# A ternary feed-forward layer: its second product from three bf16 parts of the squared activations instead of one f32 matmul

## What is computed

```python
def _ternary_weight(w, group_size):
    wb = w.astype(jnp.bfloat16)
    wg = wb.reshape(-1, group_size)
    scale = jnp.clip(jnp.mean(jnp.abs(wg), axis=-1, keepdims=True), 1e-08, None)
    q = jnp.clip(jnp.round(wg / scale), -1.0, 1.0)
    qs = (q * scale).reshape(w.shape).astype(w.dtype)
    return w + jax.lax.stop_gradient(qs - w)
...
w1 = _ternary_weight(W_fc, GROUP)             # 1024 x 256
h = jnp.einsum('bsd,hd->bsh', x, w1)
h = jnp.square(jax.nn.relu(h))                # 2048 x 1024
hn = _rms_norm(h)
w2 = _ternary_weight(W_proj, GROUP)           # 256 x 1024
return jnp.einsum('bsh,dh->bsd', hn, w2)
```

## Time and profile before

| | us |
|---|---|
| median of 3 runs (1603.28 to 1605.0) | 1603.55 |
| the profiled execution, device time | 1604.46 |
| its span from the first to the last instruction | 1602.7 |
| first `up` of the ternary layer / last `down` ends | 927.5 / 1050.3 |
| busy in the span: PE / DVE / ACT / POOL | 1513.1 / 1035.5 / 780.7 / 358.5 |

### The profile page before, as it was taken

The page is one execution under the profiler, slowest core; times in us unless marked ns, Lnnn a source line. Parts: engine busy times, 40 slices in busy tenths (PEclk is TensorE's granted clock), DMA queues, the critical chain, the costliest instruction groups (busy, mean ns, idle before and its releaser), DMA issues.

```text
span 1602.7 us, 35635 instructions
## 1 busy us (share of the span) xinstructions
PE 1513.1 (94%) x14908; PEld 943.9 (59%) x14908; DVE 1035.5 (65%) x1872; ACT 780.7 (49%) x1797; POOL 358.5 (22%) x403
## 2 busy tenths in 40 slices
PE   7999788999989999899999989999999999999998
PEld 4667454444444443445656557777777777764556
DVE  3678777788888883623436965367787878842223
ACT  2431446667767776341111153376767767732110
POOL 2322000000100003200000044335545555630000
PEclk9999889999999999999999999999999999999999
DMA  6000231000000003010000040000000020000000
GB/s 193 2 2 8 79 83 20 12 13 10 13 4 13 3 13 115 8 54 3 16 0 0 1 132 1 7 1 8 1 8 1 2 90 1 2 0 1 14 13 27
DMA packets 31823, 39.05 MB, mean 24 GB/s; under 512 B 7531, under 2 KB 26607, under 8 KB 31151
## 3 DMA queue, kind: packets, MB, share of 16 engines
q1 hardware_dynamic: 31662, 36.77, 7.9%
HBM read 23.79 MB, written 2.10 MB: 16 GB/s over the span
## 4 chain that ended last, share of the span: by engine, by line
PE 76%; DVE 11%; issue 4%; DMA 3%; ACT 3%; POOL 1%; SPq 1%; POOLq 0%; DVEq 0%; ACTq 0%
PE PS L1493 7%; PE PS L1499 7%; PE PS L1522 7%; PE PS L2742 6%; PE PS L1263 6%; PE PS L1218 6%; PE PS L1249 5%; DVE arena L1402 4%; PE PS L2249 4%; PE PS L2729 3%; PE PS L2707 3%; DMA arena<-arena 3%; PE PS L341 2%; PE PS L2572 2%; PE PS L2219 2%
## 5 line engine op out<-in xcount | busy, mean ns | idle before, releaser
L1332 ACT ACTIVATE arena<-PS 128x512 f32<-128x512 f32 (+3 forms) x640 | 313.9, 534 | 135.9 <-PE PS L1249 57.6
L1402 DVE TENSOR_REDUCE arena<-PS 128x1 f32<-128x1024 f32 (+7 forms) x320 | 326.6, 1059 | 58.1 <-PE PS L1221 41.2
L1249 PE MATMUL PS<-arena 99*32 99x512 bf16 (+3 forms) x2560 | 212.3, 352 | 1.5 <-ACT arena L1332 1.0
L1218 PE MATMUL PS<-arena 96*32 96x512 bf16 (+3 forms) x2560 | 185.2, 358 | 25.4 <-DVE arena L1402 24.4
L1263 PE MATMUL PS<-arena 128*32 128x512 f32 (+3 forms) x1280 | 150.1, 542 | 2.4 <-ACT arena L1338 1.7
L192 POOL TENSOR_TENSOR rstd<-ve,mhalf 128x4 f32<-128x4 f32 x31 | 31.7, 1023 | 498.5 <-DVE ve L220 498.4
L1218 PEld LDWEIGHTS PS<-arena 96*32 96x32 bf16 x2560 | 63.7, 98 | 103.5 <-DVE arena L1402 53.3
L2893 ACT ACTIVATE arena<-arena 128x128 f32<-128x128 f32 x256 | 122.7, 484 | 0.0
L1493 PE MATMUL PS<-XT,arena 128*128 128x512 f32 x256 | 120.4, 592 | 0.9 <-DVE arena L1730 0.9
L2742 PE MATMUL PS<-arena 128*128 128x256 f32 x512 | 121.0, 379 | 0.2
L1499 PE MATMUL PS<-XT,arena 128*128 128x512 f32 x256 | 120.3, 592 | 0.0
(11 more groups left out here) (250 smaller groups left out, 2692.7 us busy)
## 6 DMA issues: line engine op xcount, KB each, us to landing
arena<-arena SPq DMA_DIRECT2D x79, 128.0 KB, 2.4
XT<-in_L_attn_xT SPq DMA_DIRECT2D x4, 512.0 KB, 7.8
X<-in_L_attn_x SPq DMA_DIRECT2D x4, 512.0 KB, 9.5
arena<-in_L_attn_out_w SPq DMA_DIRECT2D x1, 2048.0 KB, 8.3
out<-X SPq DMA_DIRECT2D x3, 512.0 KB, 3.0
arena<-in_dmask SPq DMA_DIRECT2D x1, 1024.0 KB, 5.8
arena<-in_L_ffn_W_up SPq DMA_DIRECT2D x1, 1024.0 KB, 5.0
arena<-in_L_ffn_W_gate SPq DMA_DIRECT2D x1, 1024.0 KB, 7.5
```

The source lines that it names most:

```text
L1218: last = pe.matmul(flat[p, o:o + w], q[:, p], a.KS[0:SROWS, CH * kc:CH * kc + w], start=True, stop=kc < c)
L1249: last = pe.matmul(PS[p, b, lo:CH], keys[:, p], a.QS[0:rows, G1 * g + r, CH * c + lo:CH * (c + 1)], start=True, stop=j < TPC * c)
L1332: act.activation(a.PB[:, n % 3, r, lo:CH], PS[:, 4 + x % 3, lo:CH], ACT.Exp, scale=D0 ** -0.5).then_inc(a.e2, 1)
L1402: dve.tensor_reduce(dst, src, AX.X, ALU.max, negate=True).then_inc(a.m1, 1)
```

## The change

1. `a.down` is bf16: q * scale * sign, without the two f32 steps (subtract w, add w) that followed for the second weight matrix.
2. The f32 h of a tile is kept in 3 tile buffers instead of two whole chunks, and is split into three bf16 parts, whose sum is h: ACT makes the high part as the square of r (`l2f_high`), DVE the residual h - high (`l2f_residual`), POOL the middle part by a cast of the residual (`l2f_middle`), DVE the low part, residual - middle (`l2f_low`).
3. down is 3 bf16 matmuls in place of each f32 one. It waits for `low_s` (by halves) instead of h.
4. h(n) on DVE also waits for the square and the residual of tile n - 3; relu(n) also for the high part of tile n - 2. The DVE order is h(n), residual(n - 1), low(n - 2); the ACT order relu(n), high(n), square(n - 1); the POOL order middle(n - 1), add(n).
5. The gated layers (fourth and eighth) share one set of semaphores, with an offset `a.n0` in the counts.

```diff
@@ l2f_alloc
-    a.h = v(10 * n, [P, 2, HT, CH])
+    a.parts = [[v(at, [P, HT, CH], BF16) for at in slot] for slot in ((9216, 18944, 20992), (24640, 26688, 14400))]
+    a.h = v(12288, [P, 3, CH])
+    a.res = v(23040, [P, 2, CH])
-    a.down = a.q[:, 1, :].rearrange("p (t e) -> p t e", t=HT)
+    a.downb = v(6720, [P, n], BF16)
+    a.down = a.downb.rearrange("p (t e) -> p t e", t=HT)
@@ ternary_dve
-    elif step == 2:
+    else:
         dve.wait_ge(a.wb_s, 4 * m + 2 + half + 1)
-        last = dve.tensor_tensor(sign if m == 0 else q, q, sign, ALU.mult)
-    elif step == 3:
-        last = dve.tensor_tensor(q, q, w, ALU.subtract)
-    else:
-        last = dve.tensor_tensor(q, q, w, ALU.add)
+        last = dve.tensor_tensor(sign if m == 0 else a.downb[:, cols], q, sign, ALU.mult)
@@ l2f_relu
     if n >= 2:
         act.wait_ge(a.h_s, n - 1)
+        act.wait_ge(a.high_s, n - 1)
@@ new, and l2f_hidden
+def l2f_high(k, act, n):
+    act.wait_ge(a.r_s, n + 1)
+    if c >= 2 and it == 0:
+        act.wait_ge(k.f_ready, NC * 5 + c - 1)
+    act.activation(a.parts[c % 2][0][:, it, :], a.r[:, n % 2, :], ACT.Square).then_inc(a.high_s, 1)
+def l2f_residual(k, dve, n):
+    dve.wait_ge(a.high_s, n + 1)
+    dve.wait_ge(a.h_s, n + 1)
+    if n >= 2:
+        dve.wait_ge(a.low_s, n - 1)
+    dve.tensor_tensor(a.res[:, n % 2, :], a.h[:, n % 3, :], a.parts[c % 2][0][:, it, :], ALU.subtract).then_inc(a.res_s, 1)
+def l2f_middle(k, pool, n):
+    pool.wait_ge(a.res_s, n + 1)
+    pool.tensor_copy(a.parts[c % 2][1][:, it, :], a.res[:, n % 2, :]).then_inc(a.mid_s, 1)
+def l2f_low(k, dve, n):
+    dve.wait_ge(a.mid_s, n + 1)
+    dve.tensor_tensor(a.parts[c % 2][2][:, it, :], a.res[:, n % 2, :], a.parts[c % 2][1][:, it, :], ALU.subtract)\
+       .then_inc(a.low_s, 1)
 def l2f_hidden(k, dve, n):
     dve.wait_ge(a.r_s, n + 1)
-    if c >= 2 and it == 0:
-        dve.wait_ge(k.f_ready, NC * 5 + c - 1)
-        dve.wait_ge(a.sq_s, HT * (c - 1))
+    if n >= 3:
+        dve.wait_ge(a.sq_s, n - 2)
+        dve.wait_ge(a.res_s, n - 2)
@@ l2f_pe
     def down(c, j, half):
+        if j == 0:
+            pe.wait_ge(a.low_s, HT * c + HT // 2 * (half + 1))
         for it in range(HT // 2 * half, HT // 2 * (half + 1)):
-            last = pe.matmul(f_tile(k, j), a.h[:, c % 2, it, P * j:P * (j + 1)], a.down[:, it, :],
+            for part in range(3):
+                last = pe.matmul(f_tile(k, j), a.parts[c % 2][part][:, it, P * j:P * (j + 1)], a.down[:, it, :],
@@ l2f_act, before the loop over chunks
+    l2f_high(k, act, 0)
+    l2f_high(k, act, 1)
@@ l2f_pool, squares(c)
         for it in range(1, HT):
+            l2f_middle(k, pool, HT * c + it - 1)
             pool.wait_ge(a.sq_s, HT * c + it + 1)
@@ l2f_dve, hidden(c)
             if n >= 3:
                 l2f_hidden(k, dve, n)
+            if n >= 1:
+                l2f_residual(k, dve, n - 1)
+            if n >= 2:
+                l2f_low(k, dve, n - 2)
+            if n == HT * NC - 1:
+                l2f_residual(k, dve, n)
+                l2f_low(k, dve, n - 1)
+                l2f_low(k, dve, n)
@@ l3_front_act
-    act.wait_ge(k.l2f.h_s, HT * NC)
+    act.wait_ge(k.l2f.low_s, HT * NC)
```

More of the change, by code:

```diff
@@ L1471, in l1_dve, with glu_alloc @@
     dve.wait_ge(k.xn_done, 3 * NC)
-def glu_alloc(k, a, name, o):
+def glu_alloc(k, a, layer, o):
     a.h = k.view(o, [P, 2, HT, CH])
@@ L1480, in glu_alloc @@
     s = k.sem
-    a.g_mm, a.u_mm = s(name + "_gate_projected"), s(name + "_up_projected")
-    a.sil_s, a.h_s = s(name + "_silu"), s(name + "_hidden")
+    a.n0 = HT * NC * layer
+    a.g_mm, a.u_mm = s("gate_projected"), s("up_projected")
+    a.sil_s, a.h_s = s("gate_silu"), s("gated_hidden")
 def glu_up(k, pe, a, s, c, it):
     PS = k.PS
-    n = HT * c + it
+    n = a.n0 + HT * c + it
     if it == 0:
@@ L1516, in glu_pe @@
         else:
[L1517 removed]
+            pe.wait_ge(a.h_s, a.n0 + HT * NC)
         pe.wait_ge(k.r_done, NC * s + c)
@@ L1636, in l1f_alloc @@
     a.down = v(18944, [P, HT, E])
-    glu_alloc(k, a, "l1f", 21000)
+    glu_alloc(k, a, 0, 21000)
     a.ld = k.sem("l1f_ld")
@@ L2061, in l2f_alloc @@
     n = KT * HID
-    a.q = v(2 * n, [P, 2, n])
+    a.q = v(2 * n, [P, n])
     a.w = v(4 * n, [P, 2, n])
@@ L2094 @@
                (1, 0): (1, 0, 0), (1, 1): (1, 0, 1), (1, 6): (1, 1, 0), (1, 7): (1, 1, 1), (2, 0): (1, 2, 0), (2, 1): (1, 2, 1)}
-TERNARY_DVE = [(0, step, half) for step in range(3) for half in range(2)] + [(1, step, half) for step in range(5) for half in range(2)]
+TERNARY_DVE = [(0, step, half) for step in range(3) for half in range(2)] + [(1, step, half) for step in range(3) for half in range(2)]
 def ternary_sp(k, sp, I):
@@ L2228, in l2f_relu @@
         act.wait_ge(a.h_s, n - 1)
+        act.wait_ge(a.high_s, n - 1)
     act.activation(a.r[:, n % 2, :], k.PS[:, n % 2, :], ACT.Relu).then_inc(a.r_s, 1)
+def l2f_high(k, act, n):
+    a = k.l2f
+    c, it = n // HT, n % HT
+    act.wait_ge(a.r_s, n + 1)
[3 more added lines that the diff above has]
+def l2f_residual(k, dve, n):
+    a = k.l2f
+    c, it = n // HT, n % HT
+    dve.wait_ge(a.high_s, n + 1)
[4 more added lines that the diff above has]
+def l2f_middle(k, pool, n):
+    a = k.l2f
+    c, it = n // HT, n % HT
+    pool.wait_ge(a.res_s, n + 1)
+    if c >= 2 and it == 0:
+        pool.wait_ge(k.f_ready, NC * 5 + c - 1)
+    pool.tensor_copy(a.parts[c % 2][1][:, it, :], a.res[:, n % 2, :]).then_inc(a.mid_s, 1)
+def l2f_low(k, dve, n):
+    a = k.l2f
+    c, it = n // HT, n % HT
+    dve.wait_ge(a.mid_s, n + 1)
+    dve.tensor_tensor(a.parts[c % 2][2][:, it, :], a.res[:, n % 2, :], a.parts[c % 2][1][:, it, :], ALU.subtract)\
+       .then_inc(a.low_s, 1)
 def l2f_hidden(k, dve, n):
     a = k.l2f
-    c, it = n // HT, n % HT
     dve.wait_ge(a.r_s, n + 1)
-    if c >= 2 and it == 0:
-        dve.wait_ge(k.f_ready, NC * 5 + c - 1)
-        dve.wait_ge(a.sq_s, HT * (c - 1))
+    if n >= 3:
+        dve.wait_ge(a.sq_s, n - 2)
+        dve.wait_ge(a.res_s, n - 2)
     r = a.r[:, n % 2, :]
-    dve.tensor_tensor(a.h[:, c % 2, it, :], r, r, ALU.mult).then_inc(a.h_s, 1)
+    dve.tensor_tensor(a.h[:, n % 3, :], r, r, ALU.mult).then_inc(a.h_s, 1)
 def l2f_pe(k, pe):
@@ L2247, in down @@
     def down(c, j, half):
+        if j == 0:
+            pe.wait_ge(a.low_s, HT * c + HT // 2 * (half + 1))
         for it in range(HT // 2 * half, HT // 2 * (half + 1)):
-            last = pe.matmul(f_tile(k, j), a.h[:, c % 2, it, P * j:P * (j + 1)], a.down[:, it, :],
-                             start=it == 0, stop=it == HT - 1)
+            for part in range(3):
+                last = pe.matmul(f_tile(k, j), a.parts[c % 2][part][:, it, P * j:P * (j + 1)], a.down[:, it, :],
+                                 start=(it, part) == (0, 0), stop=(it, part) == (HT - 1, 2))
         if (j, half) == (TPC - 1, 1):
@@ L2300, in square @@
             dst = a.sq[:, it % 2, :]
-        act.activation(dst, a.h[:, c % 2, it, :], ACT.Square).then_inc(a.sq_s, 1)
+        act.activation(dst, a.h[:, n % 3, :], ACT.Square).then_inc(a.sq_s, 1)
+    l2f_high(k, act, 0)
+    l2f_high(k, act, 1)
     for c in range(NC):
@@ L2307, in l2f_act @@
                 l2f_relu(k, act, n)
+                l2f_high(k, act, n)
             if it >= 1:
@@ L2327, in squares @@
         acc = a.acc[:, c % 2, :]
+        if c >= 1:
+            l2f_middle(k, pool, HT * c - 1)
         for it in range(1, HT):
+            l2f_middle(k, pool, HT * c + it - 1)
             pool.wait_ge(a.sq_s, HT * c + it + 1)
@@ L2344, in l2f_pool @@
             squares(c + 1)
+            if c + 1 == NC - 1:
+                l2f_middle(k, pool, HT * NC - 1)
         else:
```

13 lines of the change are left out of this document (7 added, 6 removed).

## The result

The median went from 1603.41 us to 1637.32 us (four runs, 1636.89 to 1638.03), a ratio of 1.021 (95% interval 1.0192 to 1.0228): 33.9 us slower, where 1634.0 with a range of 1614 to 1656 was forecast. The profiled execution has a span of 1635.1 us, 32.4 more than before.

A forecast was written before the change was run, and what follows sets the result against it. DVE and POOL, taking turns at a shared SBUF resource, were to bound the ternary layer instead of PE: +32 for the later last down, -4 saved there, +2 for clock, 1604.5 + 30 less 0.9 = 1634 us, range 1614 to 1656.

The forecast's parts named there:

- PE's part: Ternary layer's down: 128 f32 matmuls of 432 ns become 384 bf16 ones of 107 ns, saving 14.2 us of PE.
- the weight loads: Rival in down: weight loads pace the bf16 matmuls at 205 ns, giving 1658 us; chance 0.04.
- the rival in which PE stays the bound: DVE and POOL run side by side in the ternary layer, so all 14.2 us are saved: 1589 us; chance 0.09.
- The step that decides: Ternary layer: DVE and POOL exclude each other, so a tile holds their shared resource 3.32 us against PE's 2.58.
- The second rival: POOL's cast doesn't take turns with DVE: 2.85 us a tile, 15.0 us less, 1619 us; chance 0.09.
- The sum: Held times from the third tile to low(31) total 113.9 us; last down begins at 1056.2 instead of 1024.22, +32.0.
- DVE's list is unbroken from the third tile on: DVE starts the third tile's product about 938.7, is free at 940.5, then works without a break to low(31).
- The named new waits of h(n) and relu(n): Ternary layer: these added waits are on things a full tile old, so they were given no cost.
- The last chunk: After the last down begins, faster matmuls save 4 us and the lowered clock after PE's gap costs 2.
- the third rival: PE falls to 1.2 GHz, +36 us for three chunks, 1670; chance 0.12 beyond 1655; sign: layer clock below 0.9.
- The tail doesn't wait for down: In each chunk down is done 16.3 us after its second half starts, within the 19.9 us DVE has left.
- Where the cover went: Forecast cover: PE's chunk needs 22.3 us, DVE with POOL 25.5 plus a 6.25 tail, so PE's saving counts only last.

The follow-up runs named there:

- the filler kernel: Changed kernel plus throwaway PE matmuls, 16 before the low-part wait in chunks 0 to 2 and 30 before the last down: 1633.53 us beside 1602.79, ratio 1.0189.

## Why the prediction was right

**PE's part** held: twelve bf16 matmuls take 1.31 us (109 ns each; 107 was taken), and the weight loads set no pace. The removal of the splitting gave 1591, near the 1589 of the rival in which PE stays the bound.

**The step that decides** held: DVE's two-input products and POOL's reading operations take turns, a tile at 3.29 us (3.32), the cast among them. The cast's turn, 0.47 in the sum, measured as 0.41 when it was taken away and 0.42 when it was doubled. The second rival (a free cast, 1619) falls by both runs and by the steady rows, where h takes 1.09 us beside a cast.

**The sum** was 2.5 us short at the last down: 1058.7, not 1056.2. low(31) ended at 1057.0, not 1054.4. Some 0.5 of it was there before the splitting began: the first h starts at 931.96, where it was 931.45, and so the third at 939.2, not 938.7. The step that failed is "DVE's list is unbroken from the third tile on". DVE waited 8.6 us for relu, and only the first 2.4 were in the sum; 6.2 came later. The prediction checked down(c) against DVE's tail alone. But on PE the `up` of the next tiles stands behind the down that waits for the low part, so when that down starts late and at half clock, relu is late and DVE runs out of work (2.08 us at 1005.83). The named new waits of h(n) and relu(n) aren't what held: those relus waited for PE's `up`.

Of these 6.2 us and the 0.5, some 4 were made good. A tile 0.03 us shorter than forecast explains 0.9. The rest can be read from the rows after such a wait, POOL first:

```profile
1007.06 1.80 POOL L2378 TENSOR_TENSOR arena<-arena 128x512 f32<-128x512 f32 x1 [2.84 <-ACT arena L2341]
```
```profile
1008.43 0.97 DVE L2278 TENSOR_TENSOR arena<-arena 128x512 f32<-128x512 f32 x1 [0.71 <-ACT arena L2232]
```

The addition ran mostly while DVE waited, and held h up for 0.29 us only, not for the 1.14 of the sum. Three additions (972.99, 1007.06, 1038.33) did so, and two casts (1003.21, 1035.02) ran wholly in such waits: by the held times of the sum that is 3 x 0.85 + 2 x 0.47 = 3.5 us, an estimate. How much of the 6.2 us is the clock, no run tells; the filler kernel, which gives 0.6 us back at that point, kept the clock up in one of three chunks.

The step from the profile to the median added to the miss: 0.9 was taken off for it, while the profiled execution of the changed kernel lay 0.4 below its median (1636.89 and 1637.32). Both are within what executions differ by.

**The last chunk** made good 2.1 us; -4 + 2 = -2 was forecast. The 2 us for the clock are borne out: the record of the first twelve matmuls is 2.74, and 1.49 in the filler kernel, which won 1.8 us behind that point. The sign of the third rival (PE at 1.2 GHz) was seen: the windows show 0.76 to 0.86 from 962 to 1021 us, and 0.89 over the layer, below the 0.9 that was named. Its price was not: where the clock was kept up, 2.4 to 3.8 us came back, and DVE's waits for relu behind the gaps, 6.2 us, with the 1.8 of the last chunk are all that the trace shows PE's slow starts to touch, not 36. "The tail doesn't wait for down" held: in the first three tails DVE found down done, and the only wait of the residual sum for PE, 3.1 us, is in the tail of the last chunk.

**Where the cover went.** The prediction costed the gain of PE at -3.5 us outside the last chunk's slow start, since PE waits elsewhere; with the f32 product kept the loss is 6.3 us, so somewhat more than that was in use. The trace of that kernel tells where: its last down begins 3.6 us later, as DVE waits 4.9 us longer for relu. With slower matmuls the `up` behind the waiting down is later still, the same step that failed in the sum.

## What to carry to other kernels

A saving on the engine that bounds is worth what the next bound leaves of it: here 12.7 us alone, 6.3 beside the splitting, which cost 46. Before work is put on idle-looking engines, add up the time of what they share: DVE's operations with two SBUF inputs and POOL's operations that read SBUF make one list, not two. The work can leave that list in three ways: to ACT (12.7 us here for one cast a tile), to PE, or by giving DVE one input from PSUM, if the bank's later release doesn't hold the producer. Then ask what else the late engine's list holds behind its wait: here PE's `up` stood behind a down that waited for DVE, and DVE then waited for that `up`. Putting the sum that frees PSUM first in the tail was worth some 5 us, with a long shared list and with a short one; moving the last parts alone was worth nothing (1624.59 and 1624.45).

## What was not expected of the hardware

- The length of a POOL operation doesn't tell its cost: 32 memsets of 0.52 us cost 1.3 us in all, which is not clear of noise, 32 casts of 0.60 us 12.4.
- In the steady rows the turns are strict, one instruction each. A held cast reads 1.01 us instead of 0.61, a held addition 1.71 instead of 1.27, a product 1.09 behind a cast and 1.75 behind an addition, so that in these rows a record's length names what it waited for.
- A DVE scalar_tensor_tensor with PSUM as one input takes 0.68 us, as long as the plain product, and neither holds up POOL (addition 1.26) nor is held up.
- A one-column matmul with a 128x128 weight load in bf16 is cheap enough to sum squares with: 128 of them are 7.5 us of records, and eight in a row take 0.34 us. With them in its list PE was busy for 29.8 of 30 us from 990 to 1020, and the last down still ended at 1044.2, where it was 1050.3 before.
